# A spline stage's turns in another order: down weights first, features spread, and matmuls without use between them

## The reference

```python
gate_w = spline_reconstruct(gate_cp, INTER, HIDDEN)   # 2048 x 512
up_w   = spline_reconstruct(up_cp, INTER, HIDDEN)
down_w = spline_reconstruct(down_cp, HIDDEN, INTER)
gate = jnp.einsum('bsh,ih->bsi', hidden_states, gate_w)
up   = jnp.einsum('bsh,ih->bsi', hidden_states, up_w)
inter = jax.nn.silu(gate) * up
return jnp.einsum('bsi,hi->bsh', inter, down_w)
...
x = x + tanh(g_xattn[0]) * mlstm(layernorm(x), ctx, ...)
x = x + tanh(g_ffn[0]) * ffn0(layernorm(x), gate_cp, up_cp, down_cp)
x = x + tanh(g_xattn[1]) * attention(layernorm(x), ctx, ctx)
x = x + tanh(g_ffn[1]) * ffn1(x, gate_w, up_w, down_w)      # rounded to blocks of fp8
```

## Time and profile before

| | |
|---|---|
| Median of 3 runs | 1543.31 us (1539.65 to 1543.32) |
| Profiled execution, its own time | 1553.67 us |
| Its span, first to last instruction | 1551.9 us |
| Mean granted TensorE clock | 0.913 |
| Spline stage in it | 291.3 to 364.05 us |
| First feed-forward stage begins | 364.05 us |

### The profile page before, as it was taken

How to read it: one execution, slowest core, us unless ns; L and a number is a source line. 1 busy time by engine, 2 the same in 40 slices (tenths; PEclk the granted TensorE clock), 3 DMA queues, 4 the chain that set the end, 5 groups by cost and what they waited for, 6 DMA issues and landing times. The chain is left out here.

```text
span 1551.9 us, 20163 instructions
## 1 busy us (share of the span) xinstructions
PE 1305.2 (84%) x7496; PEld 655.0 (42%) x7496; DVE 1156.8 (75%) x1527; ACT 660.5 (43%) x1047; POOL 468.5 (30%) x343
## 2 busy tenths in 40 slices
PE   5499998267798979885387888779999999999996
PEld 3278777222343434442022222234444454444443
DVE  5567778757688767994477767588888888888865
ACT  3445664356344444433254635234333334333322
POOL 0032432245555566641276597400000000000000
PEclk8789998567899999997598989999999999999999
DMA  8412231247233241225001103130000000000000
GB/s 299 136 59 66 83 109 58 76 141 231 80 112 129 99 136 68 82 95 190 27 1 43 26 14 94 56 122 8 7 7 14 7 7 7 7 7 14 7 8 14
DMA packets 59590, 106.51 MB, mean 69 GB/s; under 512 B 10863, under 2 KB 21767, under 8 KB 59388
## 3 DMA queue, kind: packets, MB, share of 16 engines
q1 hardware_dynamic: 58236, 101.34, 19.9%
q0 software_dynamic: 1280, 4.20, 0.9%
HBM read 73.47 MB, written 27.66 MB: 65 GB/s over the span
## 5 line engine op out<-in xcount | busy, mean ns | idle before, releaser
L1682 PE MATMUL FD<-W0D,HH 128*128 128x512 f16 x512 | 159.3, 394 | 11.7 <-DVE HM L1740 9.2
L2533 PE MATMUL HD<-W1H,HT 128*128 128x512 f16 x512 | 154.9, 379 | 0.0
L2336 DVE TENSOR_REDUCE NQ<-A_M 128x2 f32<-128x1024 f32 x60 | 73.3, 1222 | 54.3 <-PE A_M L2183 54.1
L1676 PE MATMUL FG<-F,W0G 97*128 97x512 f16 x324 | 84.7, 393 | 25.3 <-PEq L1043 8.7
L2479 ACT CAST OS<-SS 128x2048 f16<-128x2048 f32 x16 | 30.4, 1898 | 169.9 <-DVEq L2607 169.9
L335 ACT ACTIVATE DD<-E,TM 128x128 f32<-128x128 f32 x256 | 72.7, 370 | 68.7 <-PE E L431 67.1
L1607 POOL TENSOR_TENSOR HL<-HM,HH 128x512 f16<-128x512 f32 x48 | 76.0, 1584 | 84.9 <-ACT HH L1636 84.9
L1682 PE MATMUL FD<-W0D,HL 128*128 128x512 f16 x256 | 100.0, 391 | 0.0
L2533 PE MATMUL HD<-W1L,HT 128*128 128x512 f16 x256 | 97.0, 379 | 0.0
L2136 ACT ACTIVATE PT<-A_S,CM 128x1024 f32<-128x1024 f32 x64 | 70.9, 1111 | 58.8 <-PE A_S L2209 58.7
L2585 DVE SCALAR_TENSOR_TENSOR H<-HU,DS,SG 128x512 f32<-128x512 f32 x64 | 48.0, 751 | 61.7 <-ACT SG L2468 57.3
(11 more groups left out here) (368 smaller groups left out, 3033.8 us busy)
## 6 DMA issues: line engine op xcount, KB each, us to landing
VALP<-in_ffn_weights_dram SPq DMA_DIRECT2D x24, 512.0 KB, 3.9
VALQ<-in_ffn_weights_dram SPq DMA_DIRECT2D x24, 512.0 KB
quantised_weights<-QQ SPq DMA_DIRECT2D x24, 512.0 KB, 2.7
X<-in_x_dram SPq DMA_DIRECT2D x8, 1024.0 KB, 6.1
W1H<-quantised_weights SPq DMA_DIRECT2D x3, 2048.0 KB, 8.1
F<-features_kept SPq DMA_DIRECT2D x16, 288.0 KB
CTX<-in_ctx_dram SPq DMA_DIRECT2D x4, 1024.0 KB, 6.9
features_kept<-XQ SPq DMA_DIRECT2D x4, 1024.0 KB, 7.0
```

The lines of the kernel that those rows point to most:

```text
L1676: last = pe.matmul(banks[t][:, :], GW[rows, t, lhs, cols], F[b % 2][rows, rhs, c, :], start=(n == 0), stop=(n == 2))
L1682: last = pe.matmul(DN[c][:, :], lhs[:, at, c * P:(c + 1) * P], W2[:, i, part, :], start=(i == 0 and n == 0), stop=(i == KI - 1 and n == 2))
L2336: v.tensor_reduce(NQ[:, i % NC, at:at + 2], first_bank(g, i)[:, :, :], AX.X, ALU.max, negate=True).then_inc(mx_taken, 1)
L2533: ins = pe.matmul(DN[:, :], HT[:, q, lp, k, :], W[:, 2, i * D:(i + 1) * D], start=(i == 0 and lp == 0 and W is WH), stop=(i == KI - 1 and ...
```

## The change

The stage is written as 28 turns. Four of them (0, 1, 4, 7) make two chunks of CT each, the other 24 a unit each; the 16 down units come first, the 8 class units last. The features are spread: one transpose group a turn (turns 4 to 7 and 16 to 19), a quarter of the moments a turn (10 to 13, 22 to 25), one or two XN a turn, one `bn_stats` a turn. `quantiser.scales` moves from DVE's end to its start. SP loads RH first, each quarter with its own semaphore, and its stores of the down weights stand between the features' DMAs; the features' DMAs of batch 1 now end its stream. From turn 8 on PE issues one matmul whose result is not used before each fill (20 of them), and 12 at the end of the stage.

```diff
+CHUNK_TURNS = (0, 1, 4, 7)
+WARM_FROM, WARM_END = 8, 12
+TURN_X = {4: (0, 0), 5: (0, 1), 6: (0, 2), 7: (0, 3), 16: (1, 0), 17: (1, 1), 18: (1, 2), 19: (1, 3)}
+MOMENT_X = {10: (0, 0, 0), 11: (0, 0, 1), 12: (0, 1, 0), 13: (0, 1, 1), 22: (1, 0, 0), 23: (1, 0, 1), 24: (1, 1, 0), 25: (1, 1, 1)}
+NORM_X = {1: ((0, 0), (0, 1)), 2: ((0, 2), (0, 3)), 12: ((1, 0),), 13: ((1, 1),), 14: ((1, 2),), 15: ((1, 3),)}
...
+            def keep_down(k):
+                sp.wait_ge(wl_ready, k + 4)
+                sp.dma_start(natural.rearrange("(k p) c -> p k c", p=P)[:, k:k + 4, :],
+                             NAT[:, k:k + 4, :, :].rearrange("p k a c -> p k (a c)")).then_inc(nat_stored, 16)
             features.keep_elements(sp, 0)
+            keep_down(0)
             features.near_elements(sp, 0)
+            keep_down(4)
             features.keep_moments(sp, 0)
             features.near_moments(sp, 0)
-            for k in range(0, KI, 4):
-                sp.wait_ge(wl_ready, CLASS_UNITS + k + 4)
-                sp.dma_start(natural.rearrange("(k p) c -> p k c", p=P)[:, k:k + 4, :],
-                             NAT[:, k:k + 4, :, :].rearrange("p k a c -> p k (a c)")).then_inc(nat_stored, 16)
-                if k == 0:
-                    features.keep_elements(sp, 1)
-                    features.near_elements(sp, 1)
-                elif k == 4:
-                    features.keep_moments(sp, 1)
-                    features.near_moments(sp, 1)
+            keep_down(8)
+            keep_down(12)
+            features.keep_elements(sp, 1)
+            features.near_elements(sp, 1)
+            features.keep_moments(sp, 1)
+            features.near_moments(sp, 1)
...
+            def keep_warm(times, bank):
+                for _ in range(times):
+                    pe.matmul(bank[:, :], idh, features.CM[:, 0:2, :], start=True, stop=True)
+            for n in range(TURNS):
+                if n in TURN_X:
+                    b, k = TURN_X[n]
+                    features.transposes(pe, b, [k], T)
+                if n in MOMENT_X:
+                    b, m, part = MOMENT_X[n]
+                    features.moments(pe, b, m, range(2 * part, 2 * part + 2), T)
+                if n >= 3:
...
+                        pe.wait_ge(wf_selected, n - 2 - chunks)
+                if n >= WARM_FROM:
+                    keep_warm(1, pair[1])
...
+            pe.wait_ge(wf_selected, UNITS_W - 2)
+            keep_warm(WARM_END, banks(TURNS)[0])
```

More of the change, by code:

```diff
@@ L1045, in _ @@
         def _(sp):
[L1046 to L1049, removed]
+            sp.dma_start(PW[:, :], A["spline_powers"]).then_inc(pw_loaded, 16)
             for q in range(RUNS // QW):
@@ L1084, in high @@
                 nc.scalar.copy(weights(u, 0), WF[0:rows(u), u % 4, :]).then_inc(wh_ready, 1)
+            u = 0
             act.wait_ge(eps_ready, 1)
[L1087 to L1110, removed]
-                        act.wait_ge(features.xq_kept, 16)
-                    features.high(act, 1, range(2 * half, 2 * half + 2), T)
-                if u == MOMENT_UNIT_1:
-                    act.wait_ge(features.mq_kept, 16)
-                    features.high_moments(act, 1, T)
+            for n in range(TURNS):
+                act.wait_ge(filled, n + 1)
+                if n in CHUNK_TURNS:
+                    act.wait_ge(ct_zero, 1)
+                    for half in range(2):
+                        j, t, g = chunk(n, half)
+                        nc.scalar.copy(CT[CT_HIGH:CT_HIGH + PIECES * POLY, t, g * SUB:(g + 1) * SUB],
+                                       banks(n)[half][0:PIECES * POLY, :]).then_inc(ct_high, 1)
+                else:
+                    if u >= 4:
+                        act.wait_ge(wl_ready, u - 3)
+                    nc.scalar.copy(WF[0:rows(u), u % 4, :], banks(n)[0][0:rows(u), :]).then_inc(wf_copied, 1)
+                    if u:
+                        high(u - 1)
+                    u += 1
+                if n in SPREAD_X:
+                    first, end = SPREAD_X[n]
+                    act.wait_ge(mv_ready, end)
+                    nc.scalar.activation(SD[:, first:end], MV[:, first:end, 1], ACT.Sqrt, bias=EPS[:, 0:1]).then_inc(sd_ready, 1)
+                if n in TURN_X:
+                    b, k = TURN_X[n]
+                    if b and k == 0:
+                        act.wait_ge(features.xq_kept, 16)
+                    features.high(act, b, [k], T)
+                if n in MOMENT_X:
+                    b, m, part = MOMENT_X[n]
+                    if part:
+                        if b and m == 0:
+                            act.wait_ge(features.mq_kept, 16)
+                        features.high_moments(act, b, [m], T)
@@ L1164, in _, with spread @@
             v.memset(EPS[:, :], 1e-5).then_inc(eps_ready, 1)
+            n_eps = 1
+            def spread(m):
+                first, end = SPREAD_X[m]
+                v.wait_ge(st_ready, end)
+                for n in range(first, end):
+                    v.bn_aggr(MV[:, n, :], ST[:, n, :]).then_inc(mv_ready, 1)
             for n in range(NC):
                 v.bn_stats(ST[:, n, :], X[:, n, :]).then_inc(st_ready, 1)
-            v.wait_ge(st_ready, NC)
-            for n in range(NC):
-                v.bn_aggr(MV[:, n, :], ST[:, n, :]).then_inc(mv_ready, 1)
@@ L1718, in _ @@
                         if i == PREP_HOOKS[2]:
-                            features.moments(pe, s + 2, T)
+                            for m in range(2):
+                                features.moments(pe, s + 2, m, range(KD), T)
                     for n in range(Q_TILES):
```

266 lines of the change are left out of this document (140 added, 126 removed).

## The result

The changed kernel takes 1553.88 us (median of 20 runs, 1546.4 to 1562.8) against 1544.24 (20 runs, 1538.26 to 1552.07) for the kernel before. The ratio is 1.005, with a 95% interval of 1.0032 to 1.0069: slower, and outside the range I gave. Its profiled execution took 1552.66 us and spans 1550.4. That is less than the 1551.9 us span of the profiled execution of before, which was no typical one: its 1553.67 us lie above all 20 timed runs of that kernel. So I compare stages, not spans.

A forecast was written before the change was run, and what follows sets the result against it. SP's queue behind a round trip of features through HBM bounds the spline stage's end; E 345.1 plus 20.7 gave 365.8, 1.75 us later, next stage 0: 1545.0 us from the median 1543.31, range 1535 to 1551.5.

The forecast's parts named there:

- SP bounds the end: Spline stage's end: SP's queue of stores, landings and loads after the last down-weight store takes 20.7 us up to the barrier.
- E: Time at which SP issues the last store of down weights, after POOL's low part of unit 15; forecast 345.1.
- the term for DVE's waits: DVE's waits up to turn 19: 4 us in turns with a low part plus 2 us estimated, 6.0 together.
- At no cost in E: Turns 8 to 19: the extra matmuls hide under DVE's list, some 28 us, and add nothing before the last down-weight store.
- I take the clock as warm in the moments' turns: PE's clock was taken as high in the moments' turns and down in turns 14, 15, 20 and 21.
- The rival that PE turns cold in the spread turns: Low clock in turns 8 to 25, moments turns 2.9 us: stage ends 4 to 10 us later, 1547 to 1553; chance 0.28.
- XN at 0.9 each: DVE's four XN of batch 1, turns 12 to 15, each beside a POOL subtraction: 3.6 us together.
- Compute hidden behind SP: Turns 20 to 27 take about 12 us, so compute ends at about 356, before SP's round trip is through.
- The rival of a shorter tail: DVE's waits 2 us, XN 0.48: stage ends near 361.7, -2.4 us, 1541; chance 0.50 together with the main forecast.
- The twelve matmuls at the end: Spline stage's end: run at about 353, barrier some 10 us later, so PE is no nearer warm for the next stage.
- The next stage, nothing: Next stage up to the first down product: gathers start 10.7 us earlier, but the time changes by 0.
- That rival: Next stage: earlier gathers let the first steps run free, -9.0 us, to 1534; chance 0.22.

The follow-up runs named there:

- e_spnext: Changed kernel with SP's last two loads (moments of batch 1) moved into the next stage, behind its first three loads; 1540.78 us, ratio to before 0.9980.
- b_spnext: Kernel before with SP's loads of batch 1's moments moved into the next stage, behind its three loads; 1543.57 us, ratio 0.9983.
- a_again: The changed kernel run and profiled once more, nothing altered; 1549.24 us, ratio to the kernel before 1.0024.
- b_again: The kernel before run and profiled once more, nothing altered; 1544.11 us, ratio 1.0004.
- e_nofill: Changed kernel without its 32 matmuls without use; 1548.01 us, ratio to the kernel before 1.0032.
- e_fill20: Changed kernel with matmuls without use only from turn 20 on and the twelve at the end; 1545.88 us, ratio to the kernel before 1.0003.
- e_fill2: Changed kernel with two matmuls without use a turn instead of one; 1551.34 us, ratio to the kernel before 1.0053.
- e_gatherlate: Changed kernel with POOL's gathers held back until all 16 steps of the next stage's start are done; 1569.31 us, ratio to before 1.0155.
- e_burst: Changed kernel without matmuls without use, each batch's 16 moments matmuls in one row (turns 10 and 22); 1550.53 us, ratio to before 1.0032.
- e_nofill_spnext: Changed kernel without matmuls without use and with SP's loads of batch 1's moments moved into the next stage; 1539.29 us, ratio to before 0.9965.
- e_shift: As e_nofill_spnext, with the transposes of batch 1 one turn later (turns 17 to 20); 1540.26 us, ratio to the kernel before 0.9968.

## Why the prediction was wrong

*SP bounds the end: right, and its sum too.* The stage ended at E + 20.24, and I had E + 20.7. Term by term: store and landing of XQ 7.45 (351.55 to 359.00), forecast 7.45; loads and issue 2.41, forecast 2.37; the moments' store and landing 8.07 (361.41 to 369.48), forecast 8.8; last loads 1.54, forecast 1.60; barrier 0.77, forecast 0.45. That SP was the bound is shown by e_spnext and b_spnext. The terms of the two round trips fit in part by luck: the moments' store and its landing took 8.07 us here, 8.4 in a_again and 10.2 in b_again.

*The step that failed is E,* "E = 291.3 + 45.5 + 6.0 + 2.3 = 345.1", and in it the term for DVE's waits. E was 351.55. From the stage's start at 291.80 to the last selection of a down unit at 349.05 are 57.25 us. DVE is busy 23.92 + 4.44 + 12.77 = 41.1 of them, where my list had 45.5: the durations are right (0.72 for a selection, 0.68 for low parts and statistics), but rows of successive instructions overlap, 3.2 us in all, and my list holds the low part and the statistics of turn 19, 1.4 us, which stand behind that selection. DVE waits the other 16.1 us, where I had 6.0. They lie in three places: 5.2 us in turns 0 to 9 (29.15 - 23.92), of which 2.9 us are one wait for the second pair of chunks; 6.9 us in the moments' turns (11.35 - 4.44), where I had almost nothing; and 4.0 us in turns 14 to 19, of which 2.6 us are the wait of turn 16. Of these 10.1 us too little, 4.4 were made up by the list being too long; 0.2 more lie behind the last selection (2.5 for 2.3), and the stage began 0.5 later than I reckoned: 10.1 - 4.4 + 0.2 + 0.5 = 6.4, the error of E.

*"At no cost in E": wrong by 3 us.* The fillers were the term that I set to nothing on the ground that DVE's list covers PE. It did not: PE was the pace of these turns, so the twelve ahead of the last store cost 3.0 us, a quarter of a us each. e_nofill and e_fill20 show it, and SP's tail hands the delay on to the barrier one for one.

*"I take the clock as warm in the moments' turns"* is the ground of both, and it is what failed: the clock was 0.50 in all four of them, and at that clock PE, which fills a unit only behind its four moments, hands DVE its work late. Such a turn took 3.2 us; at the high clock one took 1.94 with two fillers (e_fill2) and 1.52 with one beside class units (the changed kernel, batch 1). By these contrasts, 1.7 us a turn in each, the four turns would have been some 6 to 7 us shorter at the clock I took, which is about the whole error of E. That is an estimate: no run has the high clock in all four, and turns behind them could take part of it back. Other waits have other roots, 2.6 us in turn 16 and 2.9 us for the second pair of chunks, but for those my 6.0 us would have been enough. The earlier trace rows held the sign already: before, in 338.10 to 343.00, PE ran twelve of batch 1's moments in 4.90 us, busy nearly all the time, at 0.50. My working there only asked what makes the clock fall, and took it for high when the moments begin.

*The rival that PE turns cold in the spread turns* had the sign, the price (4 to 10 us), the time (up to 1553, and it was 1553.88) and the cause right; its turn of 2.9 us took 3.2. Its deciding condition was wrong: the last MQ began at 359.38 and took 0.69, done by 360.1, and SP could store it only at 361.4. The delay came through E, not through the moments of batch 1. I gave it 0.28 where its ground, the turn of 2.9 us worked out at the low clock, was stronger than my ground against it, that pieces of moments with the filler make a dense PE: PE was dense, and the clock stayed low. Nor was it gaps that kept it low, as the prediction reckons beside this rival: from 318.76 to 335.00 PE had 0.4 us of them in all.

*XN at 0.9 each:* 1.18, 1.37, 0.53 and 0.61 us, 3.7 together against 3.6. The first two began beside a subtraction of POOL.

*Compute hidden behind SP:* right, but it ends at 363.81 and not at 356, for the same reason as E. The last eight turns took 12 us as forecast.

*The rival of a shorter tail:* no, since DVE's waits were longer and not shorter.

*The twelve matmuls at the end:* right that they bring nothing; PE starts the next stage at the low clock.

*The next stage, nothing:* nearly. To the first down product 0.8 us more in the undisturbed pair, and gathers that start earlier free nothing (e_gatherlate). That rival was built on slow steps seen in a single execution, which came back in none of the three later profiles of the kernel before and its two variants. The 2.7 us won back behind the first down product I had not seen.

*Carrying 10 us of difference over "as it is"* did no harm here, since the forecast was a difference.

## What to carry to other kernels

Where a stage ends in a chain of DMAs, its length is the time at which the chain can start plus the chain: find the instruction that starts it, and count every engine's work ahead of that, work without use too. First look whether the last wait of that chain is needed before the barrier at all: two DMAs moved behind it turned this loss into a small gain. An engine's list is a lower bound of a stretch, and the waits have to be worked out turn by turn by who hands what to whom; a turn in which PE has more than DVE is PE's, however idle PE is over the stage. Whether it has more is to be reckoned at the low clock unless a row shows the high one at that place. And a slow place seen in one execution wants a second profile before a mechanism is built on it.

## What the runs showed of the hardware

A PE that is busy is not for that a fast one. The changed kernel, 310.80 to 351.60 us:

```profile
310.80:351.60 40.80, 36.99 (x100) 12.36 (x99) 27.91 (x48) 21.53 (x41) 16.21 (x15) 0.50 0.49 158
```

PE was busy 36.99 of 40.80 us, between 318.76 and 335.00 with 0.4 us of gaps in all, and the granted clock stayed at 1.2 GHz. The Trainium skill's page "TensorE: Matmul & The Clock Gate", in the table of its section "Why this matters for your kernels", advises to keep TensorE continuously busy in order to get it to the full rate; this stretch does not bear that out. The clock did rise elsewhere: in e_burst behind twelve full matmuls in one row; in e_fill2 with the fourth moments' turn, at 330.5 us, after three such turns at the low clock; and in the changed kernel at 351.7 us, behind the moments of turn 22. Why there and not in the 40.8 us before stays open.

Behind the first down product the profiles fall into two groups, 43.9 to 44.0 us and 46.0 to 47.2 us to the 100th matmul. For the changed kernel and the kernel before, after their first down products in the second pair of profiles (columns as in the earlier trace rows):

```profile
401.80:445.80 44.00, 40.81 (x213) 19.82 (x214) 37.11 (x45) 17.95 (x27) 24.24 (x13) 0.97 0.11 37
```

```profile
391.50:438.20 46.70, 43.57 (x212) 20.55 (x213) 37.04 (x45) 18.00 (x27) 30.25 (x18) 0.91 0.23 69
```

The code is the same, and so is the work but for gathers that are still under way in the second, and these do not decide it: e_spnext, with the DMA share as low as in the first (0.11), took 46.7 us too. The mean granted clock is 0.97 in the first and 0.91 in the second, where it is low for longer at the start and once more on the way. So the clock's changes within this stretch go with some 2.7 us. That it is the moment at which the stage begins that decides between the two is a guess; no run varies it alone. It fell to the first group in both profiles of the changed kernel, in e_fill2, e_nofill_spnext and e_shift; whether it does so in every execution was not measured.
